# Attention in an audio tower: scores of the fifth kind and the maxima of the small bank are written by one row group each

## The reference

```python
q3, q4, q5 = (q[..., :g], q[..., g:2 * g], q[..., 2 * g:])
k3, k4, k5 = ...
v3, v4, v5 = ...
x3 = merge(_attn(q4, concat([k3, k4]), concat([v3, v4]), scale))
x4 = merge(_attn(q5, concat([k3, k5]), concat([v3, v5]), scale))
x5 = merge(_attn(q5, concat([k4, k5]), concat([v4, v5]), scale))
out = concat([x3, x4, x5], axis=2) @ w_proj.T + b_proj
```

## Time and profile before

| | |
|---|---|
| runs | 1869.96, 1871.35, 1872.80 us; median 1871.35 |
| profiled execution | 1873.42 us, span 1871.7 us |
| busy, share of the span | PE 96%, PEld 54%, DVE 80%, ACT 78%, POOL 67% |
| 500 to 1300 us (attention, steady) | PE 799.4, DVE 750.3, ACT 719.2, POOL 591.8 us busy of 800 |
| granted TensorE clock, same stretch | 1.00 |

### The profile page before, as it was taken

One profiled execution on the slowest core, in us unless ns is written; L12 is line 12 of the kernel. 1 busy time (PEld: TensorE's weight loads), 2 busy tenths in 40 slices (PEclk: granted clock), 3 DMA queues, 4 the chain that ended last, 5 costly groups with the idle time before them and its releaser, 6 DMA issues. The chain is left out here.

```text
span 1871.7 us, 59000 instructions
## 1 busy us (share of the span) xinstructions
PE 1789.6 (96%) x20032; PEld 1015.8 (54%) x20032; DVE 1495.4 (80%) x3674; ACT 1462.8 (78%) x2983; POOL 1252.7 (67%) x2306
## 2 busy tenths in 40 slices
PE   5999999599999999999999999999994999999999
PEld 3677777244444444444444444444442777777776
DVE  6887878689999999999999999999994555555554
ACT  4666666288889888988898889988884777777775
POOL 4777776467777777777777777777753565666661
PEclk9999999699999999999999999999997999999999
DMA  7344442144444444444444444444441333333332
GB/s 192 90 112 112 112 112 68 35 81 87 89 88 89 89 88 88 90 88 90 88 88 88 90 89 89 87 92 88 88 79 28 72 70 68 70 67 71 65 74 54
DMA packets 503935, 159.49 MB, mean 85 GB/s; under 512 B 452176, under 2 KB 503120, under 8 KB 503888
## 3 DMA queue, kind: packets, MB, share of 16 engines
q1 hardware_dynamic: 503888, 158.90, 40.0%
HBM read 37.26 MB, written 12.48 MB: 27 GB/s over the span
## 5 line engine op out<-in xcount | busy, mean ns | idle before, releaser
L749 DVE TENSOR_REDUCE tops<-p_maxa 128x6 f32<-128x762 f32 x512 | 482.4, 942 | 63.2 <-PE p_maxa L587 61.4
L658 PE MATMUL p_o<-probs,vn 127*32 127x256 f32 x6144 | 410.8, 385 | 0.3 <-DVE att L777 0.3
L583 PE MATMUL p_s<-qm,kt 32*128 32x256 f16 x3072 | 399.9, 276 | 1.0 <-ACT probs L704 0.4
L701 ACT ACTIVATE probs<-p_s 128x512 f32<-128x512 f32 x512 | 305.4, 596 | 108.9 <-PE p_s L583 95.1
L751 DVE TENSOR_REDUCE tops<-p_maxb 128x4 f32<-128x508 f32 x512 | 345.9, 676 | 0.0
L707 ACT ACTIVATE probs<-p_s 128x512 f32<-128x512 f32 x512 | 309.0, 603 | 0.0
L704 ACT ACTIVATE probs<-p_s 128x512 f32<-128x512 f32 x512 | 304.6, 595 | 0.3 <-PE p_s L583 0.2
L587 PE MATMUL p_maxa<-kt,qt 24*128 24x256 f16 (+1 forms) x2048 | 283.9, 250 | 17.4 <-DMA qt<-qk 8.8
L1056 DVE TENSOR_TENSOR gel_lo<-gel,gel_hi 128x512 f16<-128x512 f32 x192 | 151.0, 787 | 168.9 <-ACT gel_hi L1028 168.7
L802 POOL TENSOR_TENSOR qk<-raw,one 128x384 f16<-128x384 f32 x128 | 105.7, 826 | 220.8 <-ACT raw L725 220.8
L583 PEld LDWEIGHTS p_s<-qm,kt 32*128 32x128 f16 x3072 | 135.2, 91 | 182.6 <-issue 164.8
(11 more groups left out here) (213 smaller groups left out, 4556.9 us busy)
## 6 DMA issues: line engine op xcount, KB each, us to landing
xt_a<-in_xt SPq DMA_DIRECT2D x32, 512.0 KB, 4.4
xt_b<-in_xt SPq DMA_DIRECT2D x64, 256.0 KB, 5.2
out<-out_sb SPq DMA_DIRECT2D x32, 336.0 KB, 2.6
xt<-hx SPq DMA_TRANSPOSE x128, 2.4
kt<-qk SPq DMA_TRANSPOSE x128, 2.8
qt<-qk SPq DMA_TRANSPOSE x128, 2.4
qm<-qk SPq DMA_TRANSPOSE x128, 2.7
yt<-ay SPq DMA_TRANSPOSE x128, 2.3
```

Source lines behind the costliest of these rows:

```text
L583: return nc.tensor.matmul(o, kt[full(j), r, kind, g, :], qm[full(j), r % 2, versions, g, :], start=True, stop=True, skip_group_check=True)
L658: last = nc.tensor.matmul(p_o[32 * j:32 * j + 32, blocks, :], vn[0:NP, r, src:src + 32], probs[0:NP, r % 2, QUAD * g + j, kind * 256:(kind ...
L701: nc.scalar.activation(probs[:, r % 2, h + 1, 0:512], p_s[1][:, :, :].rearrange("p x n -> p (x n)"), ACT.Exp, scale=SCALE).then_inc(act_e1 ...
L749: nc.vector.tensor_reduce(top[:, q, pair, 4:10], p_ma[:, 0:6, 0:NP], AX.X, ALU.max, negate=True).then_inc(dve_ma[u], 1)
```

## The change

The fifth-kind scores of one call now belong to one row group: two heads, j and j + 4, of group fifth (d for u = 0, 1 and c for u = 2, 3) write p_s5. The small maxima bank p_maxb likewise gets both heads of group fourth. p_maxa gets three key kinds of query kind 5 from c into its first bank and from d into its second, as one matmul of 384 columns each. With that no bank has two writers in one call, and pe_fc and the wait on pe_half in TensorE are gone. The scratch tops has another layout, the exponential of p_s5 writes heads fifth and fifth + 4, the minima are two operations and not three, outputs waits for one exponential more, and pe_ma counts two a batch.

```diff
-        top = sb("tops", [128, 2, QUAD, 10])
+        top = sb("tops", [128, 2, 5 * HEADS])
...
                     if within(i, NB):
-                        ready(pe_ma[1], seen(i + 1))
+                        ready(pe_ma[1], seen(2 * (i + 1)))
                         ready(pe_mb[1], seen(i + 1))
...
                 a, b, c, d = lo, lo + 1, 2 - lo, 3 - lo
+                fourth, fifth = (c, d) if u < 2 else (d, c)
...
                     pe.wait_ge(dve_ma[u - 1], seen(i + 2 if u < 3 else i + 3))
-                    maximum(p_ma[:, 4:5, :], c, 1, slice(2, 3)).then_inc(pe_fc[u], 1)
+                    maximum(p_ma[:, 0:3, :], c, 1, slice(0, 3)).then_inc(pe_ma[u], 1)
+                    maximum(p_ma[:, 4:7, :], d, 1, slice(0, 3)).then_inc(pe_ma[u], 1)
+                if has_s:
+                    score(p_s[1][:, 2:4, :], b, 1, slice(0, 3, 2)).then_inc(pe_s1[u], 1)
                 if has_s:
                     pe.wait_ge(act_e5[u - 1] if u else act_e5[3], seen(i + 1 if u else i))
-                    score(p_s5[:, 0:2, :], a, 2, slice(1, 3)).then_inc(pe_half[u], 1)
+                    score(p_s5[:, 0:2, :], fifth, 2, slice(1, 3), 0)
+                    score(p_s5[:, 2:4, :], fifth, 2, slice(1, 3), 1).then_inc(pe_half[u], 1)
                 if has_m:
-                    maximum(p_ma[:, 0:2, :], d, 0, slice(0, 2))
-                if has_s:
-                    score(p_s[1][:, 2:4, :], b, 1, slice(0, 3, 2)).then_inc(pe_s1[u], 1)
-                if has_m:
-                    maximum(p_ma[:, 2:4, :], d, 1, slice(0, 2))
-                    pe.wait_ge(pe_fc[u], seen(bm + 1))
-                    maximum(p_ma[:, 5:6, :], d, 1, slice(2, 3)).then_inc(pe_ma[u], 1)
                     pe.wait_ge(dve_mb[u - 1], seen(i + 2 if u < 3 else i + 3))
-                    maximum(p_mb[:, 0:2, :], c, 0, slice(0, 2))
+                    maximum(p_mb[:, 0:2, :], fourth, 0, slice(0, 2), 0)
+                    maximum(p_mb[:, 2:4, :], fourth, 0, slice(0, 2), 1).then_inc(pe_mb[u], 1)
                 if has_s:
                     pe.wait_ge(act_e0[u - 1] if u else act_e0[3], seen(i + 1 if u else i))
                     score(p_s[0][:, 0:2, :], a, 0, slice(0, 2))
-                if has_m:
-                    maximum(p_mb[:, 2:4, :], c, 1, slice(0, 2)).then_inc(pe_mb[u], 1)
-                if has_s:
-                    pe.wait_ge(pe_half[u], seen(2 * i + 1))
-                    score(p_s5[:, 2:4, :], b, 2, slice(1, 3)).then_inc(pe_half[u], 1)
                     score(p_s[0][:, 2:4, :], a, 1, slice(0, 3, 2)).then_inc(pe_s0[u], 1)
...
+                    if kind == 2 and g == 0:
+                        pe.wait_ge(act_e5[3], seen(b + 1))
...
-                    nc.vector.tensor_reduce(top[:, q, pair, 4:10], p_ma[:, 0:6, 0:NP], AX.X, ALU.max, negate=True).then_inc(dve_ma[u], 1)
+                    nc.vector.tensor_reduce(top[:, q, 6 * pair:6 * pair + 6].rearrange("p (e k) -> p e k", e=2),
+                                            p_ma[:, :, :].rearrange("p (e k) n -> p e k n", e=2)[:, :, 0:3, 0:NP],
+                                            AX.X, ALU.max, negate=True).then_inc(dve_ma[u], 1)
...
-                    nc.vector.tensor_tensor(low[0], four[:, :, :, 0], four[:, :, :, 1], ALU.min)
-                    nc.vector.tensor_tensor(low[1], four[:, :, :, 2], fifth, ALU.min)
-                    nc.vector.tensor_tensor(low[2], four[:, :, :, 3], fifth, ALU.min).then_inc(dve_min, 1)
+                    nc.vector.tensor_tensor(low[:, 0].rearrange("p (g j) -> p g j", g=2), of4[:, 0], of4[:, 1], ALU.min)
+                    nc.vector.tensor_tensor(low[:, 1:3], of5[:, 0:2], of5[:, 2:3].broadcast_to([128, 2, HEADS]), ALU.min).then_inc(dve_min, 1)
```

More of the change, by code:

```diff
@@ L495, in attend @@
         pe_qkv, act_qk, act_v = sem("pe_qkv"), sem("act_qk"), sem("act_v")
-        pe_fc = [sem(f"pe_fc{u}") for u in range(4)]
         pe_ma = [sem(f"pe_ma{u}") for u in range(4)]
@@ L579, in products, with score, maximum @@
                 a, b, c, d = lo, lo + 1, 2 - lo, 3 - lo
+                fourth, fifth = (c, d) if u < 2 else (d, c)
                 has_s, has_m = within(i, NB), within(bm, NB)
-                def score(o, j, kind, versions):
-                    return nc.tensor.matmul(o, kt[full(j), r, kind, g, :], qm[full(j), r % 2, versions, g, :],
+                def score(o, j, kind, versions, half=g):
+                    return nc.tensor.matmul(o, kt[full(j), r, kind, half, :], qm[full(j), r % 2, versions, half, :],
                                             start=True, stop=True, skip_group_check=True)
-                def maximum(o, j, kind, cols):
-                    return nc.tensor.matmul(o, qt[short(j), rq, kind, gm, :], kt[short(j), rk, cols, gm, :],
+                def maximum(o, j, kind, cols, half=gm):
+                    return nc.tensor.matmul(o, qt[short(j), rq, kind, half, :], kt[short(j), rk, cols, half, :],
                                             start=True, stop=True, skip_group_check=True)
@@ L702, in exponentials @@
                                          scale=SCALE).then_inc(act_e1[u], 1)
-                    act.wait_ge(pe_half[u], seen(2 * i + 2))
-                    nc.scalar.activation(probs[:, r % 2, h:h + 2, 512:768],
+                    act.wait_ge(pe_half[u], seen(i + 1))
+                    fifth = (3, 1, 2, 0)[u]
+                    nc.scalar.activation(probs[:, r % 2, fifth:HEADS:QUAD, 512:768],
                                          p_s5[:, :, :].rearrange("p (h x) n -> p h (x n)", h=2), ACT.Exp, scale=SCALE).then_inc(act_e5[u], 1)
@@ L745, in maxima @@
                 bm, pair = (i + 1, 2 + (1 - u)) if u < 2 else (i + 2, 1 - (u - 2))
+                fourth = (2, 0, 3, 1)[u]
                 q = (r + 1) % 2 if u < 2 else r % 2
                 if within(bm, NB):
-                    dve.wait_ge(pe_ma[u], seen(bm + 1))
-                    nc.vector.tensor_reduce(top[:, q, pair, 4:10], p_ma[:, 0:6, 0:NP], AX.X, ALU.max, negate=True).then_inc(dve_ma[u], 1)
+                    dve.wait_ge(pe_ma[u], seen(2 * (bm + 1)))
+                    nc.vector.tensor_reduce(top[:, q, 6 * pair:6 * pair + 6].rearrange("p (e k) -> p e k", e=2),
+                                            p_ma[:, :, :].rearrange("p (e k) n -> p e k n", e=2)[:, :, 0:3, 0:NP],
+                                            AX.X, ALU.max, negate=True).then_inc(dve_ma[u], 1)
                     dve.wait_ge(pe_mb[u], seen(bm + 1))
-                    nc.vector.tensor_reduce(top[:, q, pair, 0:4], p_mb[:, :, 0:NP], AX.X, ALU.max, negate=True).then_inc(dve_mb[u], 1)
+                    nc.vector.tensor_reduce(top[:, q, 24 + 4 * fourth:28 + 4 * fourth], p_mb[:, :, 0:NP], AX.X, ALU.max, negate=True)\
+                        .then_inc(dve_mb[u], 1)
             def body(i, r):
@@ L762, in body @@
                     got = top[:, (r + 1) % 2]
-                    four = got[:, :, 0:8].rearrange("p a (e k) -> p a e k", e=2)
-                    fifth = got[:, :, 8:10]
-                    low = [slots((r + 1) % 2, 256 * x, HEADS)[:, :, 24].rearrange("p (a e) -> p a e", e=2) for x in range(3)]
-                    nc.vector.tensor_tensor(low[0], four[:, :, :, 0], four[:, :, :, 1], ALU.min)
-                    nc.vector.tensor_tensor(low[1], four[:, :, :, 2], fifth, ALU.min)
-                    nc.vector.tensor_tensor(low[2], four[:, :, :, 3], fifth, ALU.min).then_inc(dve_min, 1)
+                    of5 = got[:, 0:24].rearrange("p (h k) -> p k h", k=3)
+                    of4 = got[:, 24:40].rearrange("p (j g k) -> p k g j", g=2, k=2)
+                    low = slots((r + 1) % 2, 0, NQ)[:, :, 24].rearrange("p (x h) -> p x h", x=3)
+                    nc.vector.tensor_tensor(low[:, 0].rearrange("p (g j) -> p g j", g=2), of4[:, 0], of4[:, 1], ALU.min)
+                    nc.vector.tensor_tensor(low[:, 1:3], of5[:, 0:2], of5[:, 2:3].broadcast_to([128, 2, HEADS]), ALU.min).then_inc(dve_min, 1)
                 maxima(i, r, 2)
```

## The result

| | before | after |
|---|---|---|
| median | 1871.46 us (8 runs, 1869.75 to 1872.80) | 1876.1 us (8 runs, 1873.78 to 1880.54) |
| profiled execution | 1873.42 us, span 1871.7 us | 1876.01 us, span 1874.3 us |

The ratio is 1.0025, 95% interval 1.0016 to 1.0034. The change is slower by 4.6 us; 1865 had been forecast, with 1854 to 1880 as the range and slower as the least likely of the three directions.

A forecast was written before the change was run, and what follows sets the result against it. The ring, not busy TensorE, was taken as the bound: -0.28 - 0.16 + 0.24 = -0.20 us a round, -6.0 over 30 rounds, some -0.5 for the written-out batches, giving 1865 us (range 1854 to 1880).

The forecast's parts named there:

- The ring: Chain setting the period: M (first p_maxa matmul of u = 2), qkv, raw, kt, qt, next M; 32.46 us per four-batch round.
- (1): TensorE's products in u = 2: fewer matmuls, reordered, so qkv starts 0.50 us after M where it was 0.60.
- (2): ACT: copy raw stands behind three exponentials, 1.86 us from M; M to raw still saves 0.28 a round.
- Step (4): SyncE, between kt and qt: doubled count adds a register operation, 0.08 us three times a round, a loss of 0.24.
- Step (3): Raw to kt in the fourth batch: 2.29 us falls to 2.13 if qm is issued earlier, gaining 0.16 a round.
- The written-out batches: Batches before and after the loop, which get no register operation: credited with a gain of some 0.5 us.
- Step (5): VectorE: new reduction pattern taken as zero cost, one of three small minima dropped; off the ring, nothing enters the sum.
- Step (6): New wait of outputs(i - 1, 0, 2) on act_e5[3]: zero, since products(i, 0) already waits for the same exponential.
- Strict order on TensorE: Rival: a matmul waiting for its row group blocks all behind it; qkv at 0.74, +0.55 a round, 1888 us; 15%.
- The larger gain: Rival: register operation hidden while SyncE still works on kt; the round gains 0.44 us, 1857.5 us; 10%.

The follow-up runs named there:

- experiment 4: Two more matmuls of 192 columns in each proj on TensorE, result overwritten, added to the changed kernel: 1878.19 us, ratio 1.0034 to the kernel before.
- experiment 1: Changed kernel with SyncE waiting on VectorE's reduction (dve_ma[1], one a batch) instead of the doubled pe_ma[1], so no added register operations: 1867.65 us, ratio 0.9974.
- experiment 6: Kernel of experiment 1 with ACT's copy raw moved ahead of the third exponential in u = 2: 1894.59 us, ratio 1.0113 to the kernel before.

## Why the prediction was wrong

- **The ring** was right. Its period is M, qkv, raw, kt, qt, M; qt to M stayed 2.50, experiment 4 put work on the busiest engine and the rounds stayed the same, and experiment 1 took 0.04 to 0.13 from one SyncE interval per batch and gained 8.4 us.
- **Steps (1) and (2)**, M to qkv and ACT's floor, were right: 0.49 for 0.50, 1.87 for 1.86, -0.24 a round for -0.28.
- **Step (4)**, the register operation, failed by size: priced from the one batch that had it (+0.08), it cost 0.07 to 0.13 in the three batches that got it, and the first body's own one became 0.04 dearer: +0.32 a round instead of +0.24. One row of the old kernel was too little to price it; why it is dearest in the third batch (1.60) wasn't found, but experiment 6 has 1.58 in that batch with no operation between kt and qt.
- **Step (3)**, the late kt of the fourth batch, failed by size: 0.11 came and not 0.16, because kt in the loop's first body has a register operation of its own ahead of it. And raw to GpSimd's first split grew by 0.02 to 0.03 in each batch, 0.09 a round, together with the copy itself, which now follows an exponential directly and takes 0.46 and not 0.44; no term held this. Of -0.16, -0.02 was left.
- These are errors of 0.04, 0.14 and 0.08 us, on a sum of -0.20 made of terms of -0.28, -0.16 and +0.24. They turned its sign, but this is only 1.8 of the 4.6 us.
- **The written-out batches** are the step that failed most: credited with -0.5 us as "batches which get no register operation", they cost some +4: 2.2 to 2.7 us up to the last M and 1.2 to 2.3 behind it, where the clock had fallen. The prediction took them for rounds without the loop. They and the loop's first rounds are the batches in which code is loaded while kt and qt are sent, and a shorter program puts these loads elsewhere. The prediction's bound for them rested on no row.
- **Step (5)**, VectorE, was right: the reduction of p_maxa has a mean of 945 ns for 942. **Step (6)** too: no wait for the exponential in outputs.
- **Strict order on TensorE** fell: qkv at 0.49, p_s0 ahead of p_maxb. The Trainium skill, "TensorE: Matmul & The Clock Gate", section "The mechanism", has matmuls start in program order; this trace disagrees again, for matmuls of different row groups: p_s0 starts at 895.65 and p_maxb, ahead of it in the program, at 895.68.
- **The larger gain** is what experiment 1 reached by another way: without the operation 1867.65, for 1857.5 forecast. Of the missing 10 us, 5.5 are in the rounds (0.255 gained and not 0.44), and the tail is 3.6 to 5.7 us longer.

## What to carry to other kernels

Find the ring first, and price a change by what it puts between the ring's own instructions; a wait for a loop-dependent number with a factor of its own takes one more instruction on the waiting queue, and a wait on a semaphore that counts one a step avoids it. A forecast that sums terms of either sign near the error of each has no sign to give, and its chances should say so. Where code runs once, behind a loop, its instruction loads share the DMA engines with the data, so a change of program length alone can lengthen or shorten such a stretch by several microseconds (77.9 to 83.5 us here): compare the loop's rounds before believing a small difference in the total.

## What the runs showed of the hardware

- Matmuls on different row groups of TensorE started out of program order where, by the spacing of the starts, the one ahead waited for its own row group (both p_s0 ahead of p_maxb at 895.68).
- A register operation of SyncE between two issues costs 0.07 to 0.13 us there; behind qt, one in each body cost 0.02 to 0.04 us a round.
- An instruction packet of 16 KB beside a DMA transpose went with issues of up to 2.7 us instead of 1.2, and with qt to M of 2.6 to 4.1 us instead of 2.5; beside one of 8 KB alone it was 3.2 to 3.3 us.
- TensorE's granted clock fell to 0.5 (1.2 GHz) for 3.4 us, 1.7 us after an idle time of 1.58 us had ended; in the loop, with idle times of 0.2 us, it stayed at 1.00.
